# Three width-8 attentions without loops, their tokens read from the norm's tile

## What is computed

```python
x = x + L0_attn(layernorm(x)); x = x + L0_ffn(layernorm(x))      # 16 heads of width 64; gated MLP
x = x + L1_attn(layernorm(x)); x = x + L1_ffn(layernorm(x))      # 16 heads of width 8  ("a1"); gated MLP
x = x + L2_attn(layernorm(x)); x = x + L2_ffn(layernorm(x))      # Fourier attention; 4 experts ("a2")
x = x + L3_attn(layernorm(x)); x = x + L3_ffn(layernorm(x))      # rotary, 16 heads of width 8 ("a3"); sign MLP

# a1: softmax over all 256 keys, 16 heads of width 8
q, k, v = split(x @ W_qkv + b_qkv)
out = softmax(q k^T, axis=-1) / sqrt(128) @ v @ W_out + b_out
# a2: a router picks 2 of 4 experts per token; each expert is such an attention among its own tokens
for e in range(4):
    att = where(valid_key, q_e k_e^T * 0.5, -1e9)
    out += gate[:, e] * (softmax(att) @ v_e @ wo[e] + bo[e])
# a3: as a1, with q and k turned by rotary angles and a scale of 8 ** -0.5
```

## Time and profile before

| | us |
|---|---|
| three runs | 2452.52, 2454.14, 2454.62 |
| median | 2454.14 |
| the profiled execution | 2456.93 |
| its span (first to last instruction) | 2455.2 |
| mean granted TensorE clock over the span | 0.926 |

### The profile page before, as it was taken

How to read it: one execution, slowest core, us unless ns; L and a number is a source line. 1 busy time by engine, 2 the same in 40 slices (tenths; PEclk the granted TensorE clock), 3 DMA queues, 4 the chain that set the end, 5 groups by cost and what they waited for, 6 DMA issues and landing times. The chain is left out here.

```text
span 2455.2 us, 67707 instructions
## 1 busy us (share of the span) xinstructions
PE 2145.5 (87%) x21623; PEld 1268.2 (52%) x21637; DVE 1822.4 (74%) x4585; ACT 1465.5 (60%) x3719; POOL 678.3 (28%) x1207
## 2 busy tenths in 40 slices
PE   4999999986999886665899999999999968998688
PEld 3777777753455454432445555555555534444355
DVE  6778877745899357773889999999999756775554
ACT  2555555532688523222778888888888826776331
POOL 3111111101442000002343444444444235660110
PEclk9999999997899897766899999999999968999899
DMA  4000000002343000002434444444444213330000
GB/s 148 9 2 2 2 2 2 2 1 65 118 129 107 2 1 1 1 0 67 130 116 129 129 129 129 129 130 130 128 131 128 67 62 109 107 113 31 5 14 18
DMA packets 195122, 167.12 MB, mean 68 GB/s; under 512 B 15382, under 2 KB 173944, under 8 KB 194936
## 3 DMA queue, kind: packets, MB, share of 16 engines
q1 hardware_dynamic: 194936, 164.74, 21.2%
HBM read 85.36 MB, written 77.63 MB: 66 GB/s over the span
## 5 line engine op out<-in xcount | busy, mean ns | idle before, releaser
L777 DVE TENSOR_REDUCE a_rowmax<-a_psS 128x2 f32<-128x512 f32 x1536 | 962.1, 683 | 189.3 <-PE a_psS L569 184.8
L715 ACT ACTIVATE a_probs<-a_psT 128x512 f32<-128x512 f32 x1536 | 829.6, 602 | 208.9 <-PE a_psT L576 208.5
L569 PE MATMUL a_psS<-stackk,stackq 49*128 49x256 bf16 x3072 | 505.2, 282 | 49.8 <-DMA stackq<-a_negmaxT 15.5
L576 PE MATMUL a_psT<-stackq,stackk 51*128 51x256 bf16 x3072 | 481.2, 275 | 3.2 <-ACT a_probs L715 2.9
L621 PE MATMUL a_psO<-a_probs,values 128*32 128x256 f32 x6144 | 415.5, 388 | 2.1 <-ACT a_probs L715 2.1
L569 PEld LDWEIGHTS a_psS<-stackk,stackq 49*128 49x128 bf16 x3072 | 222.3, 96 | 307.4 <-DVE a_rowmax L777 121.1
L621 PEld LDWEIGHTS a_psO<-a_probs,values 128*32 128x32 f32 x6144 | 161.3, 109 | 147.4 <-issue 57.5
L576 PEld LDWEIGHTS a_psT<-stackq,stackk 51*128 51x128 bf16 x3072 | 218.2, 95 | 24.8 <-ACT a_probs L715 12.1
L1055 ACT ACTIVATE a_probs<-a_psS,a_negmax 128x256 f32<-128x256 f32 x256 | 121.7, 475 | 182.0 <-DVE a_negmax L1079 182.0
L836 POOL COPY a_xcur<-xT 128x256 f32 (+1 forms) x96 | 38.1, 396 | 581.0 <-ACT values L733 390.9
L941 POOL TENSOR_TENSOR a_vr<-a_v,a_rsum 128x256 f32<-128x256 f32 x128 | 79.5, 621 | 388.8 <-DVE a_rsum L1125 335.8
(11 more groups left out here) (297 smaller groups left out, 3911.7 us busy)
## 6 DMA issues: line engine op xcount, KB each, us to landing
a_scratch<-a_parts SPq DMA_DIRECT2D x192, 192.0 KB, 2.3
stackq<-a_scratch SPq DMA_DIRECT2D x192, 192.0 KB
stackk<-a_scratch SPq DMA_DIRECT2D x192, 192.0 KB
a_scratch<-a_parts SPq DMA_DIRECT2D x192, 128.0 KB, 2.3
a_scratch<-a_parts SPq DMA_DIRECT2D x192, 64.0 KB, 1.9
stackq<-a_negmaxT SPq DMA_DIRECT2D x192, 8.0 KB
out<-x SPq DMA_DIRECT2D x8, 256.0 KB, 2.3
stackk<-mask_dram SPq DMA_DIRECT2D x64, 8.0 KB
```

Of the source, the lines that this page charges most:

```text
L569: return pe.matmul(psS[score_bank(s, u)[0]][:, t * SEQ:(t + 1) * SEQ], stackq[r:r + MAX_ROW, b, pr, t * P:(t + 1) * P], stackk[r:r + MAX_R ...
L576: return pe.matmul(psT[shifted_bank(s, u)[0]][:, t * SEQ:(t + 1) * SEQ], stackk[r:r + ZERO_ROW, b, pr, t * P:(t + 1) * P], stackq[r:r + ZE ...
L715: act.activation(probs[:, h, :], psT[shifted_bank(s, u)[0]][:, :], ACT.Exp, scale=w.exp_scale).then_inc(exp_done, 1)
L777: dve.tensor_reduce(rowmax[:, s.parity(1), u, :], psS[score_bank(s, u)[0]][:, :].rearrange("p (t k) -> p t k", t=2), AX_X, ALU.max).then_i ...
```

## The change

All three attentions are written out without a loop: every step is built with constants for what its waits compare with and for its addresses. The copy `xcur`, its semaphore and GpSimd's `tokens` go; the projections read the norm's transposed tile `m.xT16` directly, and where a norm is woven in (a1, a3), TensorE waits for the group that holds the job's sequence.

```diff
-    jobs, unroll, first = BATCHES * weights, 4, 4
-    plan = Plan(jobs, weights, unroll, first, rounds=(jobs - LEAD - first) // unroll, drain=2)
+    jobs, unroll = BATCHES * weights, 4
+    plan = Plan(jobs, weights, unroll, first=jobs, rounds=0, drain=2)
...
-        xcur = sb("xcur", [P, 4, SEQ])
...
-        ones_set, mask_cleared, tokens_ready = sem("ones_set"), sem("mask_cleared"), sem("tokens_ready")
+        ones_set, mask_cleared = sem("ones_set"), sem("mask_cleared")
...
             def project_qk(s, kind, wq, wk):
-                pe.wait_ge(tokens_ready, s.n(3, 1, 1))
+                if normed:
+                    norm.wait(pe, s.batch(3) // 2)
                 ps, full = fill(s, kind, 3)
-                xc = xcur[:, s.quarter(3), :]
+                xc = m.xT16[:, s.batch(3), :]
...
-                    mm = pe.matmul(ps[:, t * D:(t + 1) * D], xcur[:, s.quarter(0), t * P:(t + 1) * P],
+                    mm = pe.matmul(ps[:, t * D:(t + 1) * D], m.xT16[:, s.batch(0), t * P:(t + 1) * P],
...
-            def tokens(s):
-                if s.known(4, 4):
-                    wait_taken_alone(pool, s, "v", 0, pool_passed)
-                if normed and s.turns is None and s.at < first:
-                    wait_alone(pool, norm.xT_written, s.batch(4) // 2 + 1 if s.at + 1 < first else GROUPS, pool_passed)
-                pool.tensor_copy(xcur[:, s.quarter(4), :], m.xT16[:, s.batch(4), :]).then_inc(tokens_ready, 1)
...
-                if s.has(4):
-                    tokens(s)
```

## The result

The changed kernel takes 2465.17 us (median of 7), the kernel before 2454.62 in the same runs: a ratio of 1.0041, interval 1.0028 to 1.0054. It is slower by 10.5 us where the prediction's sum gave 33. The direction and the way the time is lost were as forecast; its size was less than a third.

A forecast was written before the change was run, and what follows sets the result against it. In a2's loop TensorE and VectorE hand score tiles to each other and neither has slack. Token copies -4, loop control -5 and code +42 sum to +33 on the profiled 2456.93, 2489.9, or 2487 as median; range 2440 to 2530.

The forecast's parts named there:

- The mechanism: a2: code packets on the data's DMA engines delay SyncE's saves, then the max rows, so TensorE waits; 75 more q8 packets.
- The price of a step's code: a1 to a3: 60 steps fetch code anew at 0.70 us each, +42; ends +14 (0.24 each) and +111.
- turned registers into constants: TensorE's queue: some 16 register operations of 32 ns per step for line 592 go; costed at 0.
- Loop control: a1 to a3: 17 returns to the loop's head saved at 0.3 us each, -5; ends 0 and -7.6.
- Token copies: Starts of a1, a2 and a3: GpSimd's copies no longer delay projections, -0.4 twice and -3, sum -4; ends 0 and -8.6.
- the first scores: a3: a sign of being right, its first scores some 3 us earlier counted from the stage's start.
- A: Rival: packets hidden, written-out steps run as the loop's do, only -4 - 5 counts; 2445 us; chance 0.22.
- B: Rival: TensorE's queue was the bound, without register operations all steps run at 11.66 us; -42, 2412 us; chance 0.06.
- C: Rival: all written-out steps go as a2's first pass did; +102, 2556 us; chance 0.08.
- D: Rival: terms cancel, code term at its lower end or below, +5 at most; 2450 to 2459 us; chance 0.12.

The follow-up runs named there:

- e3: Changed kernel with a2's mask row issued by SyncE ahead of its wait for the saves, against the kernel before: 2450.14 us, ratio 0.9990.
- e7: Kernel before with a2's loop of 28 steps per round and 2 rounds, against the kernel before: 2491.39 us, ratio 1.0161.
- e10: Changed kernel with 8 more long-met waits per a2 step on SyncE (0.5 us), against the kernel before: 2482.07 us, ratio 1.0111.
- e13: Changed kernel with 16 more long-met waits per a2 step on SyncE (1.04 us), against the kernel before: 2505.02 us, ratio 1.0187.
- e4: Kernel before with one more 16 KB DRAM-to-DRAM DMA per a2 step, issued by GpSimd, against the kernel before: 2458.31 us, ratio 1.0019.
- e8: Kernel before with a2's loop of 8 steps per round instead of 4, against the kernel before: 2526.39 us, ratio 1.0303.
- e11: Kernel before with 8 more long-met waits per a2 step on SyncE, against the kernel before: 2461.87 us, ratio 1.0034.
- e12: The same kernel as e10, run once more for a profile of one more execution: 2492.79 us, no ratio.
- e5: Kernel before with a2's mask row issued ahead of SyncE's wait for the saves, against the kernel before: 2444.74 us, ratio 0.9973.

## Why the forecast was right in direction and wrong in size

*The mechanism* held step by step: 74 more packets of q8 (75 forecast), 65 of them inside a2's 52 steps; late saves, late max rows, a stall of TensorE at the slot that waits for them; lateness of which e3 takes away 10 of 23 us while the packets stay.

*The price of a step's code* is the step that failed: "So 60 x 0.70 = +42". a2's 52 steps were to lose 36 us by it and gain 4 by the loop's returns; they lost 14.8 net, so the term measured about 19 us there, 0.36 per step. It has two faults. The first is the form of the code. The 0.70 came from the loops' first passes, which are code in the looped form, with its register arithmetic on SyncE. In that form fetched code does cost as much: e7 took 41.7 us more than before in the 52 steps, 0.80 each, one slow return included. But the change also turned registers into constants. I looked at that on TensorE's queue alone and put it at 0; on SyncE's queue it gave the chain 0.5 us of room, and e10 to e13 show that room moves the price. It is the larger part of the difference to e7, and not shown to be all of it.

The second is the sample. a2's first pass was two stalls of over 2 us in four steps, both of the kind that loses the clock. The same steps of the loop's first pass, with the same 5 packets of q8 or one more, took 52.7, 50.7, 52.6 and 53.2 us in e4, e7, e8 and e11, against 56.81:
```profile
1217.28:1270.01 52.73, 50.06 (x600) 26.57 (x596) 44.99 (x83) 41.99 (x93) 22.55 (x45) 0.97 0.38 119
```
```profile
1212.24:1262.90 50.66, 48.29 (x600) 25.99 (x596) 44.98 (x82) 41.80 (x93) 20.39 (x41) 1.00 0.41 129
```
```profile
1215.98:1268.62 52.64, 48.46 (x600) 25.87 (x596) 45.08 (x82) 42.00 (x93) 20.38 (x41) 1.00 0.41 126
```
```profile
1217.26:1270.48 53.22, 49.99 (x600) 26.28 (x596) 45.14 (x82) 42.05 (x93) 20.38 (x41) 0.97 0.38 117
```
With their mean of 52.3 the same rule gives 0.38 per step, +23, and a sum of +14, near what was measured. So it is in part luck that 0.70 is near e7's 0.80: one long first pass of a2 made up for the steps of a1 and a3, which lose less. A smaller fault: q14 rose by 38 packets, not 75, since constants make the other engines' code shorter.

*First passes* were left out of the sum as if they stayed. a2's took 6.0 us less, which is mostly that the one before was long. Room isn't seen in them: with 0.5 and 1 us less of it (e10, e12, e13) the four steps took 51.1, 50.9 and 50.7 us, against 50.80.

*Loop control* (-5) was near: e5's steps are 12.20 with every fourth at 12.45, the written-out step is 12.19, which makes 3 to 4 us for a2.

*Token copies* were to give 4 us. In a3 the second job's projection came 3.7 us earlier, counted from the stage's first, as forecast, and nearly all of it was given back at once: the first scores, which were to come 3 us earlier, came 0.4 us earlier. They had waited 0.7 us for the norm and now wait for stack loads, first before, then after:
```profile
2008.67 0.58 PE L569 MATMUL a_psS<-stackk,stackq 49*128 49x256 bf16 x2 [0.73 <-ACT xT L317]
```
```profile
2015.48 0.58 PE L569 MATMUL a_psS<-stackk,stackq 49*128 49x256 bf16 x2 [4.09 <-DMA stackk<-a_scratch]
```
I had asked what is queued behind the projection on TensorE, and not when the stack loads would be there.

*The rivals.* A (packets hidden) fell: 15 steps are late. B fell: no step came near 11.66, the written-out ones are 12.19. C fell: the step behind a late one is on time in all cases but one, and 35 of the 65 packets cost next to nothing. D's time, 2459 at most, is nearer to 2465 than the forecast's 2487, but its condition isn't met: the code term came out above its lower end, 0.36 per step against 0.24, and loss and gain did not cancel.

## What to carry to other kernels

Unrolling is paid in DMA time: once the code of a loop doesn't stay in the engines, it arrives in large packets over the engines that carry the data. Before unrolling, look for the DMA chain that ends just in time, count its room on the issuing engine's own queue, register arithmetic included, and move an independent DMA into a wait of that chain, as e5 does. A price that is read from one disturbed first pass holds only for that form of the code and that much room, and four steps of one execution are too few to read it from. Ask also when in a step the packets come: only those that meet the saves cost here.

## What was not expected of the hardware

A loop of four steps ran 13 returns without one packet of code and 0.2 us of branch on TensorE; one of eight steps fetched all of its code in each round and took 3.8 us to return. TensorE's code comes in packets of 16 KB on one queue, the others' in 8 KB on another; 22 more of the small ones cost nothing here. A packet of 16 KB lasted 1.05 us, and beside one the last of 96 reports of the saves' landing came 1.7 us after the other 95.
